# Odd tiles' probabilities turned by VectorE in 32x32 blocks and by two transfers, even tiles' x put into the output bank by ScalarE

## What is computed

```python
Q = (img_embed @ Wq).reshape(B, -1, H, D).transpose(0, 2, 1, 3)
K = (sent_embed @ Wk).reshape(B, -1, H, D).transpose(0, 2, 1, 3)
V = (sent_embed @ Wv).reshape(B, -1, H, D).transpose(0, 2, 1, 3)
score = jnp.einsum('bhqd,bhkd->bhqk', Q, K) / math.sqrt(D)
attn = jax.nn.softmax(jnp.where(mask, score, -jnp.inf), axis=-1)
ctx = jnp.einsum('bhqk,bhkd->bqhd', attn, V).reshape(B, -1, H * D)
out = ctx @ Wo + img_embed
return (out - mu) * jax.lax.rsqrt(var + EPS) * gamma + beta
```

## Time and profile before

| | us |
|---|---|
| median of 3 runs | 347.9 (347.08 to 348.27) |
| the profiled execution, its own time | 347.34 |
| its span, first to last instruction | 345.5 |
| TensorE busy | 339.5 |
| VectorE busy | 277.8 |
| ScalarE busy | 248.7 |
| GpSimd busy | 241.6 |

### The profile page before, as it was taken

One profiled execution on the slowest core, in us unless ns is written; L12 is line 12 of the kernel. 1 busy time (PEld: TensorE's weight loads), 2 busy tenths in 40 slices (PEclk: granted clock), 3 DMA queues, 4 the chain that ended last, 5 costly groups with the idle time before them and its releaser, 6 DMA issues.

```text
span 345.5 us, 7100 instructions
## 1 busy us (share of the span) xinstructions
PE 339.5 (98%) x2328; PEld 309.0 (89%) x2328; DVE 277.8 (80%) x513; ACT 248.7 (72%) x806; POOL 241.6 (70%) x252
## 2 busy tenths in 40 slices
PE   8999999999999999999999999999999999999994
PEld 6999999988988899889988998899889988998884
DVE  2159999497878777989798798897987988979896
ACT  3267764596788799787697787876877778768460
POOL 2045650599998989987968869779688696794243
PEclk9999999999999999999999999999999999999999
DMA  8999778799751180134244053242440531412012
GB/s 250 410 420 351 277 229 326 272 336 308 250 212 29 29 289 2 56 130 156 72 138 155 32 183 106 79 157 73 139 155 30 184 109 75 155 64 91 30 53 101
DMA packets 19996, 56.25 MB, mean 163 GB/s; under 512 B 1884, under 2 KB 3420, under 8 KB 18040
## 3 DMA queue, kind: packets, MB, share of 16 engines
q1 hardware_dynamic: 19096, 54.80, 44.6%
q10 hardware_dynamic: 864, 1.00, 1.0%
HBM read 46.98 MB, written 8.39 MB: 160 GB/s over the span
## 4 chain that ended last, share of the span: by engine, by line
PE 88%; ACT 5%; DVE 2%; POOL 2%; issue 2%; DVEq 0%; POOLq 0%; ACTq 0%
PE pair L837 29%; PE pair L750 22%; PE pair L623 12%; PE pair L616 11%; PE pair L725 5%; PE pair L814 4%; PE pair L740 2%; ACT prob L1024 2%; ACT prob L1033 1%; PE pair L855 1%; PE pair L860 1%; PE pair L817 1%; POOL xo_lo L1606 1%; POOL xo_lo L1612 1%; ACT w_out_hi L936 0%
## 5 line engine op out<-in xcount | busy, mean ns | idle before, releaser
L837 PE MATMUL pair<-vw_hi,pt_hi 128*128 128x512 f32 (+1 forms) x155 | 62.2, 402 | 0.0
L837 PE MATMUL pair<-vw_hi,pt_lo 128*128 128x512 f32 (+1 forms) x155 | 61.0, 394 | 0.0
L837 PE MATMUL pair<-vw_lo,pt_hi 128*128 128x512 f32 (+1 forms) x155 | 60.8, 392 | 0.0
L1559 POOL TENSOR_TENSOR out_sb<-centred,beta_sb 128x512 f32<-128x512 f32 x30 | 38.8, 1295 | 30.5 <-ACT centred L1084 30.4
L1033 ACT ACTIVATE prob<-c,neg_max 128x77 f32<-128x77 f32 x128 | 43.9, 346 | 0.0
L1612 POOL TENSOR_TENSOR xo_lo<-x_sum,xo_hi 128x512 fp32r<-128x512 f32 x32 | 42.4, 1330 | 0.0
L750 PE MATMUL pair<-a_hi,xo_hi 128*128 128x304 f32 x128 | 40.1, 313 | 0.0
L1077 ACT ACTIVATE pt_hi<-pair 128x640 fp32r<-128x640 f32 x32 | 22.5, 703 | 22.4 <-PE pair L817 22.4
L750 PE MATMUL pair<-a_lo,xo_hi 128*128 128x304 f32 x128 | 38.5, 301 | 0.0
L750 PE MATMUL pair<-a_hi,xo_lo 128*128 128x304 f32 x128 | 38.5, 301 | 0.0
L1631 POOL TENSOR_TENSOR w_proj_lo<-w_proj,w_proj_hi 128x768 fp32r<-128x768 f32 x10 | 18.4, 1860 | 27.9 <-ACT w_proj_hi L928 27.9
(11 more groups left out here) (136 smaller groups left out, 1047.3 us busy)
## 6 DMA issues: line engine op xcount, KB each, us to landing
w_out<-wo SPq DMA_DIRECT2D x8, 1024.0 KB, 5.1
xt_in<-x_tiles SPq DMA_DIRECT2D x16, 512.0 KB, 3.9
x_in<-x_rows SPq DMA_DIRECT2D x16, 512.0 KB, 4.8
out<-out_sb SPq DMA_DIRECT2D x31, 256.0 KB, 2.2
w_out<-wq_t SPq DMA_DIRECT2D x7, 1024.0 KB, 7.9
w_proj<-wv SPq DMA_DIRECT2D x8, 768.0 KB, 5.0
w_proj<-wk SPq DMA_DIRECT2D x6, 768.0 KB, 9.5
w_out<-wq_t SPq DMA_DIRECT2D x2, 512.0 KB, 7.7
```

The source lines that it names most:

```text
L837: mm = pe.matmul(ps_out[:, i % 2, 0:s.model], ps[0:rows, j, :], v[0:rows, j, b, :], start=(j == 0 and n == 0), stop=(j == s.key_t - 1 and ...
L1559: pool.tensor_tensor(out_sb[i % OUT_RING][:, :], centred[i % 2][:, :], beta_sb[:, :], ALU.add)\
```

## The change

Tiles 3, 5, ..., 29 are no longer transposed by TensorE. VectorE transposes their 128 x 640 probabilities in blocks of 32 x 32 (`turn_blocks`, right behind `normalise(a - 1)`; `prob_rest` of odd tiles is widened to 128 columns and zeroed once). One transfer writes the blocks to memory (128 partitions, four pieces of 640 bytes each), and four transfers read them back so that block rows and columns change places. ScalarE copies the result into the transpose bank (`take_turned`), after which both halves are taken as before; the split of odd tiles is moved on both engines. For even tiles ScalarE puts x into the output bank ahead of the matmuls, which add to it, and VectorE's residual of even tiles is gone. The load of x rows waits for both users of the buffer. SyncE's loop is written anew. The core of the diff (waits of the first tiles are left out):

```diff
@@ ScalarE
+            def take_turned(i):
+                act.wait_ge(ld_turn, STRIPS * DMA_INC * (turn_no(i) + 1))
+                act.wait_ge(dve_pt_lo, i)
+                src = prob_t[:, :, :, :].rearrange("p a t q -> p t a q")
+                act.activation(pt_blocks.rearrange("p t (a q) -> p t a q", q=STRIP), src, ACT.Copy).then_inc(act_turn, 1)
             def split_pt(i):
-                act.wait_ge(pe_pt, i + 1)
+                if by_transfer(i):
+                    act.wait_ge(act_turn, turn_no(i) + 1)
+                else:
+                    act.wait_ge(pe_pt, pt_no(i) + 1)
...
+            def x_even(i):
+                c = i // CHUNK
+                act.wait_ge(ld_x[c % X_RING], use(c, X_RING))
...
+                    act.wait_ge(dve_centred, i - 1)
+                act.activation(ps_out[:, 0, 0:s.model], x_in[c % X_RING][:, 0, :], ACT.Copy).then_inc(act_x_even, 1)
@@ ScalarE, loop over p
-                split_pt(a - 1)
+                x_even(a - 2)
                 exps_first(p)
                 scale(a - 3)
+                take_turned(a - 1)
+                split_pt(a - 1)
                 exps_second(p)
@@ VectorE
+            def turn_blocks(i):
+                dve.wait_ge(dve_prob, i + 1)
...
+                    dve.wait_ge(kept_turn, DMA_INC * turn_no(i))
+                to = blocks_t[:, :, :, :].rearrange("p g t q -> p t g q")
+                main = mains_of(prob[1][:, :]).rearrange("p t (g k) -> p t g k", k=STRIP)
+                dve.transpose(to[:, 0:s.key_t - 1, :, :], main)
+                dve.transpose(to[:, s.key_t - 1, :, :], prob_rest[1][:, :].rearrange("p (g k) -> p g k", k=STRIP))\
+                   .then_inc(dve_turn, 1)
@@ VectorE, loop over p
                     combine_first(p)
                     normalise(a - 1)
+                    turn_blocks(a - 1)
                     split_pt(a - 2)
                 residual(a - 3)
                 moments(a - 3)
@@
                 combine_c12(p)
-                split_pt(a - 1)
                 combine_c21(p)
                 normalise(a)
-                residual(a - 2)
+                split_pt(a - 1)
                 moments(a - 2)
@@ TensorE, out_rows
+                even = i % 2 == 0
                 pe.wait_ge(dve_pt_lo, i + 1)
-                if i >= 2:
+                if even:
+                    pe.wait_ge(act_x_even, i // 2 + 1)
+                elif i >= 2:
                     pe.wait_ge(dve_centred, i - 1)
...
-                                       start=(j == 0 and n == 0),
+                                       start=(not even and j == 0 and n == 0),
@@ TensorE, loop over p
                 transpose_prob(a - 2)
                 out_rows(a - 3)
-                transpose_prob(a - 1)
                 product_s3(p)
@@ SyncE
+            def keep_blocks(i):
+                sp.wait_ge(dve_turn, turn_no(i) + 1)
...
+                sp.dma_start(turned.rearrange("g a j f -> (a j) g f"),
+                             blocks_t[:, :, :, :].rearrange("p g t q -> p g (t q)")).then_inc(kept_turn, DMA_INC)
+            def load_turned(i):
+                sp.wait_ge(kept_turn, DMA_INC * (turn_no(i) + 1))
...
+                for g in range(STRIPS):
+                    sp.dma_start(prob_t[g * STRIP:(g + 1) * STRIP, :, :, :].rearrange("p a t q -> p a (t q)"),
+                                 turned[g].rearrange("a j f -> j a f")).then_inc(ld_turn, DMA_INC)
@@ SyncE, loop
+            for p in range(2, NPAIRS):
+                a = 2 * p
+                keep_blocks(a - 1)
+                store(a - 4)
+                load_turned(a - 1)
+                if p + 2 < CHUNKS:
+                    load_xt(p + 2)
+                if X_RING <= p + 1 < CHUNKS:
+                    load_x(p + 1)
+                store(a - 3)
```

More of the change, by code:

```diff
@@ L132, in build @@
             lt("gap1", [P, 256])
-            lt("gap3", [P, s.row + P])
+            blocks_t = lt("blocks_t", [P, STRIPS, s.key_t, STRIP])
+            lt("gap3", [P, s.row + P - s.key_t * P])
             x_in = [lt(f"x_in{n}", [P, CHUNK, s.model]) for n in range(X_RING)]
@@ L183, in build @@
         c12 = sb("c12", [P, s.half])
-        prob_rest = [sb(f"prob_rest{n}", [P, s.rest_rows]) for n in range(2)]
-        sb("gap2", [P, 288 - 2 * s.rest_rows])
+        prob_rest = [sb("prob_rest0", [P, s.rest_rows]), sb("prob_rest1", [P, P])]
+        sb("gap2", [P, 288 - s.rest_rows - P])
         prob1 = sb("prob1", [P, s.row])
@@ L498, in t_done, with by_transfer, turn_no, pt_no @@
             return sum(len(steps_of(m)) for m, _ in ahead)
+        def by_transfer(i):
+            return i % 2 == 1 and FIRST_TURNED <= i <= T - 3
+        def turn_no(i):
+            return (i - FIRST_TURNED) // 2
+        def pt_no(i):
+            return sum(not by_transfer(j) for j in range(i))
         def batch_of(p):
@@ L587, in _ @@
                 load_x(c)
[L588 to L593, removed]
+            for c in range(XT_RING, XT_RING + 2):
+                load_xt(c)
+            for p in range(2, NPAIRS):
[8 more added lines that the diff above has]
+                store(a - 3)
+            for t in range(T - 4, T):
                 if t == LAST:
@@ L597, in _ @@
                       .then_inc(stored[t % OUT_RING], DMA_INC)
[L598 to L603, removed]
+                else:
+                    store(t)
             for n in range(OUT_RING):
@@ L837, in out_rows @@
                         mm = pe.matmul(ps_out[:, i % 2, 0:s.model], ps[0:rows, j, :], v[0:rows, j, b, :],
[L838 to L839 removed]
+                                       start=(not even and j == 0 and n == 0),
+                                       stop=(j == s.key_t - 1 and n == len(passes) - 1), skip_group_check=even)
                 mm.then_inc(pe_out, 1)
@@ L1357, in normalise @@
                 scales = inv.rearrange("p (j n) -> p j n", n=2).unsqueeze(3)
-                if i >= 2:
-                    dve.wait_ge(pe_pt, i - 1)
-                dve.tensor_tensor(prob_rest[i % 2][:, :].rearrange("p (j n k) -> p j n k", n=2, k=s.rest),
+                if i >= 2 and by_transfer(i - 2):
+                    dve.wait_ge(dve_turn, turn_no(i - 2) + 1)
+                elif i >= 2:
+                    dve.wait_ge(pe_pt, pt_no(i - 2) + 1)
+                dve.tensor_tensor(prob_rest[i % 2][:, 0:s.rest_rows].rearrange("p (j n k) -> p j n k", n=2, k=s.rest),
                                   ends_of(prob[i % 2][:, :], H // 2), scales.to_broadcast([P, H // 2, 2, s.rest]), ALU.mult)
```

49 lines of the change are left out of this document (38 added, 11 removed).

## The result

The changed kernel takes 359.19 us (median of 3 runs, 359.13 to 359.82) against 347.9 before: ratio 1.032, interval 1.0297 to 1.0344. It is slower by 11.3 us; 357.5 was forecast, with a range of 350 to 372. The profiled execution took 359.13 us, its span 357.3, at a granted clock of 0.999.

The account below looks back on a forecast made before the run. TensorE, 98% busy, was taken to bound the kernel before; 2.25 us added to a ring with 1.63 slack would make pairs of 14.52. 347.34 + 9.4 + 0.8 = 357.5 us, range 350 to 372.

Parts of the forecast that it names:

- The ring: Loop between ScalarE and VectorE, exponentials through copy_s1, add_u2 and max_c11 to the next exponentials: 14.52 us a pair, chance 0.60.
- Turn: VectorE's two block transposes behind normalise(a - 1): 0.80 us added to the ring, plus 0.11 for the dependency.
- copy: ScalarE's copy of 640 elements into the transpose bank, take_turned: 0.73 us added to the ring, with the dependent split's 0.03.
- moved split: ScalarE's split_pt(a - 1), moved from idle time to behind take_turned, ahead of the odd exponentials: 0.61 us added to the ring.
- the ring's own work: Pair of 13.90 us less VectorE's two waits for TensorE, 1.38 and 0.17, and 0.08 of overlap: 12.27 us.
- Transfers: One write and four loads on SyncE's queue, awaited by take_turned: 6.45 us, just hidden in 6.9 available.
- the rival: The transfers set the pair instead: at 7.9 us, pairs of 15.5 and 370.5 us in all; chance 0.20.
- The load of x tiles: In SyncE's order, moved behind the write, a store and four loads: some 3 us later against its reader, no cost.
- the sum: Whole-kernel total: 347.34 us, plus 9.4 up to the last pair's first exponentials, plus 0.8 after: 357.5 us.
- The start: Up to the loop's first exponentials: 0.9 us later, with everything ahead of tile 3 unchanged.
- The tail: After the loop, ScalarE's extra 1.34 us ahead of tile 29's output rows, partly covered: 0.8 us, between 0 and 1.3.
- Its slack under TensorE: Room in the ring before it, rather than TensorE's 13.90 us a pair, sets the time: 1.63 us.

Follow-up runs that it names:

- the last kernel above: Changed kernel without the copy into the transpose bank, tiles 5 to 25 turned, both maxima first, ScalarE's x for tiles 2 to 28 only: 345.59 us, ratio 0.993.
- the kernel with both maxima first: Changed kernel with VectorE's order combine_c22, max_c11, residual, combine_c12 with its maximum, then moments and centre of tile a - 3: 354.4 us, ratio 1.0185.
- The kernel with the x part alone: Kernel before, with only ScalarE putting even tiles' x into the output bank and VectorE's even residual gone: 349.17 us, ratio 1.0026.
- The kernel with the unused turn: Kernel before, with VectorE block transposes that nothing reads and the odd split moved behind the even exponentials: 356.92 us, ratio 1.0249.

## Why the prediction was right

**The ring.** Predicted 14.52, measured 14.37. Turn: 0.91 with its dependency, measured 1.54 - 0.60 = 0.94; copy 0.73, measured 0.71; moved split 0.61, measured 0.60. The sum of these is 2.25 both ways. 12.27 + 2.25 was 0.15 too much, so the ring's own work is 12.12. The difference can be read from the rows. From the residual to the maximum the prediction had 252.18 to 254.40 less the wait of 0.17, 2.05; in the changed kernel it is 1.96 (259.29 to 261.25), as this second wait, too, had the 0.08 of overlap to give back that was taken off only once. The low half's step is 0.71 for 0.74, and from `copy_s1` to `add_u2` pass 0.49 for 0.53.

**TensorE.** Predicted idle 1.1 us a pair at `combine_c22`. The profile names 0.82 in the pair shown. By starts the wait costs more: from 260.35 to 261.48 are 1.13 us and to the next start 0.21, where a product without a wait steps by 0.14. That is 1.06 in all and leaves 13.31 for TensorE's own work, against 13.35; the 13.26 to 13.31 of the last kernel above say the same.

**The transposes.** Their prices on record from the Trainium skill (VectorE: DVE Perf Modes, "The three transpose paths") are for 128x128 in bf16, and the tiles here are f32. Part of the distance to the 0.11 us of each TensorE transpose in a stream, and to VectorE's 0.27 us for 128x128, may be the type; no run here separates it.

**Transfers.** Predicted 6.45 us with 6.9 available. The write landed in 2.5 (2.75 predicted), the loads in 2.1 by the median (2.2) and 3.4 at most; from the end of a turn at 244.29 to the last landing some 6.0. Hidden in full in 12 of 14 pairs, as forecast. The reason given against the rival was sound, that VectorE and ScalarE hold the loop anyway: once they don't, as in the kernel with both maxima first, the rival is what happens.

**The load of x tiles** went from 239.97 to 248.68 against a reader that went from 247.90 to 254.81: 6.1 us for a landing of at most 4.9 in the loop. It came 1.8 us later against its reader, where 3 was the estimate. Nothing waited for it.

**What the sum hid.** The profiled execution is 11.8 us longer where 10.2 was the sum: first exponentials at 145.99 (145.3 predicted), those of the last pair at 334.24 (333.8), and the rest 23.06 against 21.09.

- The start lost 1.58, not 0.9. "Everything ahead of tile 3 is unchanged" was wrong: ScalarE's copy of x is made for tile 0 too, where ScalarE has no idle time to cover it:

```profile
128.90 0.59 ACT L1158 ACTIVATE pair<-x_in 128x512 f32<-128x512 f32 x1
129.42 0.63 ACT L1030 ACTIVATE vw_hi<-rest_rows 104x512 fp32r<-104x512 f32 x1
```

  It pushes pair 1's first exponentials from 131.28 to 131.81 and `copy_s1` from 138.22 to 138.75; 0.53 and 0.94 make 1.47 of the 1.58. The kernel with the x part alone shows the same 0.51, without a turn or a moved split.
- Thirteen pairs took 188.25, 14.48 each: 14.37 where undisturbed, 14.77 at the change of batch and 14.67 and 14.91 where the loads came 0.17 and 0.42 late. By luck that met the 14.5 of the sum: the ring's 0.15 too much and the disturbed pairs, which the sum left out, nearly cancel.
- The tail lost 1.97, not 0.8, outside the bounds of 0 to 1.3 that the prediction gave. It was argued from ScalarE's extra 1.34 ahead of tile 29's output rows. TensorE's timeline shows two waits instead:

```profile
340.21 0.63 PE L860 MATMUL pair<-identity,prob 128*128 128x128 f32 x4 [1.71 <-DVE pt_lo L1455]
345.31 0.47 PE L886 MATMUL pair<-vw_hi,pt_hi 128*128 128x512 f32 x1 [0.36 <-ACT pair L1158]
```

Tile 30's transposes wait for tile 29's low half, as both use the transpose bank; tile 30's x waits for `centre(28)`. The 0.8 for the tail was the term most under-sized.

**A weak point in the argument.** "Its slack under TensorE is 1.63 us a pair, and whatever enters the ring beyond that sets the time" was true of that ring alone. The kernel with the unused turn shows a second ring with a slack of some 1.0 us in the kernel before. The change removes it with the transposes of odd tiles, so the forecast stood, but for the kernel before the rule was wrong: it would have called 1.55 us free that cost 9.

## What to carry to other kernels

Work taken from the busiest engine is worth at most the slack of the next loop between engines, and the work given to that loop counts in full beyond it; here 0.55 us a pair left TensorE and 2.25 entered a loop with 1.63 to spare. List every loop that closes once a round, those through a shared buffer or bank too, and give each its slack: a reordering that shortens one stops at the next, as the reorderings here did. Cost the first and the last round by themselves, because the bound engine doesn't cover anything there.

## What the runs showed of the hardware

VectorE's subtraction of 128x640 with both operands in SBUF took 1.40 us beside a GpSimd sum and 0.82 without one, as shown above; the copy into PSUM, 0.71 us of the ring, also kept VectorE clear of this. The block transposes, with one operand in SBUF, took 0.71 and 0.27 us although a GpSimd instruction was running when they began, in all 14 of the larger and 13 of the smaller. A block transpose costs VectorE about what a plain operation of its size costs: 0.71 us for 128x512 and 0.27 for 128x128, 14 times each within 0.004 us, where the scaling takes 0.68 for 512 and 0.26 for 104 elements. The transfer in pieces of 640 bytes was no slower for its size than the stores of whole tiles: 320 KB written in 2.5 us, 256 KB in 2.1. That the loads spread from 1.9 to 3.4 us was not followed up. After waits of TensorE of 1.89, 3.29 and 3.80 us, in the tails of three of the kernels, its granted clock was 0.50 to 0.52 in stretches of 2 us, and 128x512 matmuls stepped by 0.43 us instead of 0.23. In the tail of the changed kernel it stayed at 1.00.
